# A recurrence over 2048 steps on one core: set-up reordered, first and last chunk's products spread

## What is computed

```python
xn = layernorm(x)
z  = layernorm(xn) * ln_g + ln_b
z  = z + depthwise_conv3(z)                       # over time
gate, ig = split(z @ gate_w.T + gate_b)
Bm = (z * sigmoid(ig)) @ B_w.T + B_b              # 64 states
Cm = z @ C_w.T + C_b
A_bar = expm(dt_A * A)                            # 64 x 64
for t in range(2048):
    s = layernorm(s @ A_bar + Bm[t]) * st_g + st_b
    y[t] = Cm[t] * s
g = silu(xn @ W.T + b + (xn @ V_r) @ C.T)
out = x + (y @ D_w.T + D_b) * sigmoid(gate) * g
```

## Time and profile before

| | us |
|---|---|
| median of 3 runs (lowest, highest) | 2497.48 (2494.24, 2498.33) |
| the profiled execution | 2498.52 |
| its span, first to last instruction | 2496.7 |
| busy: PE, DVE, POOL, ACT | 2455.1, 2187.8, 1239.9, 1013.1 |

### The profile page before, as it was taken

The page is one execution under the profiler, slowest core; times in us unless marked ns, Lnnn a source line. Parts: engine busy times, 40 slices in busy tenths (PEclk is TensorE's granted clock), DMA queues, the critical chain, the costliest instruction groups (busy, mean ns, idle before and its releaser), DMA issues.

```text
span 2496.7 us, 42418 instructions
## 1 busy us (share of the span) xinstructions
PE 2455.1 (98%) x10031; PEld 1313.3 (53%) x10031; DVE 2187.8 (88%) x10934; ACT 1013.1 (41%) x1859; POOL 1239.9 (50%) x2433
## 2 busy tenths in 40 slices
PE   8999999999999999999999999999999999999996
PEld 4555555555555555555555555555555555555544
DVE  5788889988889988899988899888899888899886
ACT  4444433444434443434443434443334444344310
POOL 1445555545555545555445555445555455555443
PEclk9999999999999999999999999999999999999997
DMA  3112212122112122112122112122112122111121
GB/s 112 24 43 59 51 39 53 48 52 60 45 39 58 49 51 60 43 41 55 47 55 60 43 41 55 48 55 60 42 41 52 49 58 59 39 44 52 31 59 36
DMA packets 99542, 125.14 MB, mean 50 GB/s; under 512 B 31967, under 2 KB 48479, under 8 KB 99296
## 3 DMA queue, kind: packets, MB, share of 16 engines
q1 hardware_dynamic: 98560, 121.25, 19.7%
q10 hardware_dynamic: 736, 1.18, 0.2%
HBM read 71.96 MB, written 33.55 MB: 42 GB/s over the span
## 4 chain that ended last, share of the span: by engine, by line
PE 43%; POOL 28%; DVE 20%; issue 8%; ACT 0%; DMA 0%; SPq 0%; POOLq 0%; DVEq 0%; ACTq 0%
POOL dw L428 25%; PE bank L1243 9%; DVE wq L934 8%; PE bank L1232 7%; PE bank L1222 7%; DVE dw L961 6%; DVE dw L947 5%; PE bank L1309 5%; PE bank L1310 4%; POOL ln L455 3%; PE bank L1253 2%; PE bank L1271 2%; PE bank L1262 2%; PE bank L1182 1%; PE bank L1198 1%
## 5 line engine op out<-in xcount | busy, mean ns | idle before, releaser
L428 POOL TENSOR_TENSOR dw<-q,minus_half 8x1 f32<-8x1 f32 x2048 | 1085.7, 530 | 1190.4 <-DVE wq L934 1157.4
L1309 PEld LDWEIGHTS bank<-Mscan,wT 128*65 128x65 f32 x2046 | 228.0, 136 | 618.1 <-issue 607.0
L1232 PE MATMUL bank<-xnorm,gateT 128*128 128x512 f32 x1024 | 507.5, 594 | 0.9 <-DVE sgT L887 0.9
L934 DVE SCALAR_TENSOR_TENSOR wq<-dw 8x65 f32<-8x65 f32 x2048 | 443.2, 216 | 70.2
L1243 PE MATMUL bank<-xnorm,gateT 128*128 128x512 f32 x1024 | 503.3, 597 | 0.0
L1222 PE MATMUL bank<-xnT,WT 128*128 128x512 f32 x1024 | 494.5, 593 | 0.0
L1309 PE MATMUL bank<-Mscan,wT 128*65 128x128 f32 x2046 | 404.4, 279 | 14.0 <-DVE wT L964 11.8
L1310 PE MATMUL bank<-Mscan,wT 128*65 128x128 f32 x2046 | 392.4, 274 | 0.0
L961 DVE SCALAR_TENSOR_TENSOR dw<-dw 8x64 f32<-8x64 f32 x1024 | 279.3, 273 | 111.4 <-POOL dw L428 85.7
L951 DVE SCALAR_TENSOR_TENSOR dw<-bank,dw 8x128 f32<-8x128 f32 x1024 | 342.7, 335 | 12.8 <-PE bank L1310 10.4
L947 DVE SCALAR_TENSOR_TENSOR dw<-dw 8x64 f32<-8x64 f32 x1024 | 279.4, 273 | 77.4 <-POOL dw L428 75.6
(11 more groups left out here) (188 smaller groups left out, 2746.0 us busy)
## 6 DMA issues: line engine op xcount, KB each, us to landing
xc<-in_x SPq DMA_DIRECT2D x252, 128.0 KB, 2.8
xa<-in_x SPq DMA_DIRECT2D x252, 128.0 KB, 2.7
out<-o SPq DMA_DIRECT2D x248, 128.0 KB, 2.4
dw<-dtok SPq DMA_DIRECT2D x127, 96.0 KB
wtok<-dw SPq DMA_DIRECT2D x128, 33.0 KB
gateT<-in_gateT SPq DMA_DIRECT2D x1, 2048.0 KB
WT<-in_WT SPq DMA_DIRECT2D x1, 1024.0 KB, 7.6
xa<-in_x SPq DMA_DIRECT2D x4, 256.0 KB
```

Of the source, the lines that this page charges most:

```text
L428: nc.gpsimd.tensor_tensor(dw[0:B, t, CR:CR + 1], q[:], minus_half[0:B, 0:1], ALU.pow).then_inc(s["r_ready"], 1)
L934: V.scalar_tensor_tensor(out=wq[:], in0=w_eps, scalar=1.0 / S, in1=w_eps, op0=ALU.mult, op1=ALU.mult, accum_out=q[:]).then_inc(s["q_ready" ...
L1232: ins = mm(mbank["gate", m][:], gateT[:, k, P * m:P * m + P], xnorm[p][:, k, :], start=(k == 0), stop=(k == KH - 1))
L1309: mm(scanP[0:WIDE, 0:2 * S], wT[:, 0:WIDE], Mscan[:, 0, :], start=True, stop=False)
```

## The change

In set-up, x's statistics for chunk 0 leave the series and follow its last link; two operations on the small vectors, a memset and a copy move behind the fourth squaring; W's additions take other places; the low-rank products and the halo's transposes swap banks, so that the transposes of z wait for W's additions in place of the halo's copies; the last two of x's four transposes and their copies move behind the squarings. The second to fourth groups of first slots move into steps 0 and 1 of chunk 0, the small product of the first quarter to step 1, b_rest to steps 2 to 5, fill_d to step 6; the other places of chunk 0 move by two (the gate's stay at 44 to 59). On ACT normalise_z(2) moves ahead of copy_dT_rest. In the last chunk last_mm of the third quarter is cut in two halves at steps 57 and 58, and the last quarter's output goes out in two halves, the first on SP's queue, the second on ACT's. Nothing is computed differently.

```diff
-PE_Z_FIRST = (6, 6, 8, 8)
-V_CONV_FIRST = range(9, 25)
+PE_Z_FIRST = (8, 8, 10, 10)
+V_CONV_FIRST = range(11, 27)
-PE_FFN_FIRST = range(5, 21)
-PE_C_FIRST = (21, 22, 23, 24)
-PE_X_FIRST = (18, 18, 23, 23)
-PE_IG_FIRST = range(25, 41)
-PE_B_FIRST = (41, 42, 43, 45)
-PE_D_FIRST = (48, 51, 54, 58)
-V_XG_FIRST = (31, 32, 35, 36, 39, 40, 43, 44)
+PE_FFN_FIRST = range(7, 23)
+PE_C_FIRST = (23, 24, 25, 26)
+PE_X_FIRST = (18, 18, 25, 25)
+PE_IG_FIRST = range(27, 43)
+PE_B_FIRST = (43, 44, 45, 47)
+PE_D_FIRST = (50, 53, 56, 60)
+V_XG_FIRST = (33, 34, 37, 38, 41, 42, 45, 46)
-PE_BREST0 = (0, 0, 1, 1)
-PE_D0 = (3, 3, 3)
+PE_SLOTS0 = (0, 0, 1)
+PE_BREST0 = (2, 3, 4, 5)
+PE_D0 = (6, 6, 6)
-DVE_WPRIME = (2, 3, 3, 4)
+DVE_WPRIME = (1, 1, 2, 3)
-PE_X0 = (10, 10, 12, 12)
+PE_X0 = (10, 10)
-        wbank = [banks[3 + k] for k in range(KH)]
-        hbank = [banks[n] for n in (7, 1, 2, 3)]
+        wbank = [banks[n] for n in (3, 4, 1, 2)]
+        hbank = [banks[n] for n in (7, 3, 4, 5)]
...
-            send_last(3)
+            sp.wait_ge(s["last_add"], 2 * NQ - 1)
+            sp.dma_start(out[:, T - QT:T, 0:H // 2], z[:, NQ - 1, 0:H // 2]).then_inc(s["last_out"], 16)
...
-            for k in range(KH):
+            for k in range(2):
                 copy_xnT(0, k)
             for m in range(KH):
                 input_gate(0, m)
+            for k in range(2, KH):
+                copy_xnT(0, k)
...
             for u in range(DIRECT // 2):
                 copy_first_slots(u)
+            copy_dtok_first()
+            normalise_z(2)
             copy_dT_rest()
-            copy_dtok_first()
+            copy_dtok_second()
             copy_dtok(0, 1)
-            normalise_z(2)
...
+            act.wait_ge(s["last_add"], 2 * NQ)
+            act.dma_start(out[:, T - QT:T, H // 2:H], z[:, NQ - 1, H // 2:H]).then_inc(s["last_out"], 16)
...
-            bn_stats(1, 0, 0)
             dve.wait_ge(s["pe_setup"], 6)
...
-            bn_stats(1, 0, 1)
             dve.wait_ge(s["pe_setup"], 7)
             link(V.tensor_copy(XX[:, 1, :], scanP[0:S, 7 * S:8 * S]))
-            bn_stats(1, 1, 0)
-            bn_stats(1, 1, 1)
-            vec_op(5)
-            vec_op(6)
-            V.memset(ys[S:WIDE, :], 0.5)
-            V.tensor_copy(Dcat[0:S, 0:S], ident[0:S, 0:S])
+            for j in range(2):
+                for h in range(2):
+                    bn_stats(1, j, h)
             for n in range(SQUARINGS):
...
                 if n == 0:
                     for h in range(2):
                         bn_stats(1, 2, h)
+                    bn_stats(1, 3, 0)
                 if n == 1:
-                    for h in range(2):
-                        bn_stats(1, 3, h)
+                    bn_stats(1, 3, 1)
                     aggregate(1)
+                if n == 3:
+                    vec_op(5)
+                    vec_op(6)
+                    V.memset(ys[S:WIDE, :], 0.5)
+                    V.tensor_copy(Dcat[0:S, 0:S], ident[0:S, 0:S])
...
             def fill_z(c, k, i, middle):
                 wait_for(pe, "z_done", NJ, c + 1, NJ)
-                wait_bank(pe, T_USERS, "z", k, i, middle)
+                if c == 0 and k < 2:
+                    pe.wait_ge(s["wprime_done"], k + 3)
+                else:
+                    wait_bank(pe, T_USERS, "z", k, i, middle)
...
-            pe.wait_ge(s["xnT_done"], KH)
+            pe.wait_ge(s["xnT_done"], 2)
...
             mm(scanP[0:S, 4 * S:5 * S], MT[:], M, start=True, stop=True).then_inc(s["pe_setup"], 1)
+            pe.wait_ge(s["dve_setup"], SETUP_M + 4)
+            for k in range(2, KH):
+                fill_x(0, k, -1, False)
             b_first(3)
...
-            for u in range(1, DIRECT // 2):
-                first_slots(u)
...
+                            for u in range(1, DIRECT // 2):
+                                if PE_SLOTS0[u - 1] == t:
+                                    first_slots(u)
+                            if t == 1:
                                 first_quarter_rest()
...
-                        if t in PE_SSM_LAST:
+                        if t in PE_SSM_LAST[:2]:
                             last_mm(PE_SSM_LAST.index(t))
+                        if t == PE_SSM_LAST[2]:
+                            last_mm(2, range(KH // 2))
+                        if t == PE_SSM_LAST[2] + 1:
+                            last_mm(2, range(KH // 2, KH))
```

More of the change, by code:

```diff
@@ L105 @@
 PE_Z0 = (4, 4, 5, 5)
-DVE_STATS1 = (0, 0, 1, 1)
-DVE_WPRIME = (2, 3, 3, 4)
+DVE_WPRIME = (1, 1, 2, 3)
 DVE_CONV = (5, 6, 7, 9)
@@ L196, in build @@
         names = """held consts vec_ready bt_in gate_in vc_in weights_in halo_in xa_in xc_in dve_cleared pool_cleared pe_setup dve_setup halo_zeroed wprime_mm wprime_done bt_steps
-            hmean_done hvar_done b0_mm dT0_done dfirst_mm dfirst_done q0_done
+            hmean_done hvar_done b0_mm dT0_done dfirst_mm dfirst_done q0_mm q0_done
             p_ready r_ready w_ready q_ready wT_ready rest_ready a_ready
@@ L410, in _ @@
             send_last(2)
-            send_last(3)
+            sp.wait_ge(s["last_add"], 2 * NQ - 1)
+            sp.dma_start(out[:, T - QT:T, 0:H // 2], z[:, NQ - 1, 0:H // 2]).then_inc(s["last_out"], 16)
             for name in OUT:
                 sp.wait_ge(s[name], 16 * BJ * LAST)
-            sp.wait_ge(s["last_out"], 16 * NQ)
+            sp.wait_ge(s["last_out"], 16 * (NQ + 1))
         @block.gpsimd
@@ L617, in copy_dtok_first, with copy_dtok_second @@
             def copy_dtok_first():
-                act.wait_ge(s["dfill"], 1)
+                act.wait_ge(s["q0_mm"], 1)
                 nc.scalar.copy(dtok[0:B * (QT - DIRECT), 0, :], tbank["d", 0][0:B * (QT - DIRECT), 0:3 * S]
                                ).then_inc(s["q0_done"], 1)
+            def copy_dtok_second():
+                act.wait_ge(s["dfill"], 1)
                 nc.scalar.copy(dtok[:, 1, :], tbank["d", 0][:, 3 * S:6 * S]).then_inc(s["dtok_done"], 1)
@@ L683, in _ @@
             act.wait_ge(s["vec_ready"], VEC_OPS)
-            act.wait_ge(s["wprime_done"], KH)
             for k in range(3):
@@ L1204, in fill_d @@
                     wait_for(pe, "dT_done", 1, c, 1)
+                if c == 0 and q == 1:
+                    pe.wait_ge(s["q0_done"], 1)
                 if q % 2 == 0 or c == 0:
@@ L1281, in last_fill_w, with last_mm @@
                 tp(last_w[q][:, 0:P], wr[:, q, :], ident[:]).then_inc(s["last_wT"], 1)
-            def last_mm(q):
+            def last_mm(q, blocks=range(KH)):
                 wait_for(pe, "last_ys", 1, q, 1)
@@ L1289, in last_mm @@
                     wait_for(pe, "last_sg", 2, q - 2, 2)
-                for m in range(KH):
+                for m in blocks:
                     ins = mm(last_ssm[q][:, P * m:P * (m + 1)], DT[:, P * m:P * (m + 1)], ys[:, P * q:P * (q + 1)],
                              start=True, stop=True)
-                ins.then_inc(s["last_ssm"], 1)
+                if blocks[-1] == KH - 1:
+                    ins.then_inc(s["last_ssm"], 1)
             def last_fill_o(q):
@@ L1315, in fill_halo @@
                 pe.wait_ge(s["z_done"], NJ)
-                if k == 3:
-                    pe.wait_ge(s["wprime_done"], 1)
+                if k in (1, 2):
+                    pe.wait_ge(s["wprime_done"], k)
                 for j in range(NJ):
@@ L1414, in _ @@
             mm(scanP[0:B, 0:2 * S], vT[:], Dcat[0:S, S:], start=True, stop=True).then_inc(s["p_ready"], 1)
-            for u in range(1, DIRECT // 2):
-                first_slots(u)
             def first_quarter_rest():
                 mm(tbank["d", 0][0:B * (QT - DIRECT), 0:3 * S], dT[:, B * DIRECT:P], Dcat[:],
-                   start=True, stop=True)
+                   start=True, stop=True).then_inc(s["q0_mm"], 1)
             def iteration(i, p, parts, middle):
@@ L1436, in iteration @@
                                     b_rest(k)
-                            if PE_D0[0] == t:
+                            for u in range(1, DIRECT // 2):
+                                if PE_SLOTS0[u - 1] == t:
+                                    first_slots(u)
+                            if t == 1:
                                 first_quarter_rest()
```

## The result

| us | kernel before | changed kernel |
|---|---|---|
| median (lowest, highest), 10 runs each | 2495.17 (2493.03, 2498.33) | 2489.02 (2487.98, 2491.04) |
| the profiled execution | 2498.52 | 2491.04 |
| its span | 2496.7 | 2489.2 |

The ratio is 0.9973 with the interval 0.9965 to 0.9981: 6.15 us less, 0.25%. The ten runs of the kernel before have a median 2.3 lower than the three that the prediction had.

A forecast was written before the change was run, and what follows sets the result against it. The prediction took the recurrence of 2048 steps as the bound, no engine alone. Its terms, 1.15 + 0.87 + 3.5 - 1.45 - 0.1 + 0.95 + 0.4 = 5.3, off the profiled 2498.52 gave 2493.2 us, range 2489.5 to 2497.5.

The forecast's parts named there:

- Statistics and banks: Set-up: earlier statistics of x and swapped banks bring make_y to 27.2; gain 1.15 us (bounds 0.3 and 1.3).
- x's transposes: Set-up: one pair of transposes moves from the squarings into PE's 1.17 wait; gain 0.87 us (bounds 0.2 and 0.9).
- Chunk 0's start: Loop start: slots run fast and DVE's 3.67 wait at t=2 goes; gain 3.5 us, 2.1 if the clock falls.
- rival B: Loop start: the clock falls again there, 1.4 us lost, giving 2494.6; chance 0.18.
- Chunk 0's crowding: Chunk 0: B's products for chunk 1 overfill the pairs of t=44 and 46; loss 1.45 us (bounds 1.1 and 1.7).
- the last gate's tanh behind fill_d at t=60: Chunk 0: fill_d and its copy push this tanh on ACT onto its due time at t=61; loss 0.1 us.
- Last chunk: Steps 57 to 59: halving the eight records removes DVE's 0.99 wait; gain 0.95 us (bounds 0.6 and 1.0).
- Tail: Final output: the first half's transfer starts earlier; gain 0.4 us (bounds a loss of 0.5 and a gain of 1.5).
- case (A): Whole kernel: the terms as summed, with the same clock luck, 2493.2 us with 1.5 either way; chance 0.41.
- Rival C: Squarings in set-up: the clock comes back sooner, worth 1.7 to at most 3.3 us, giving 2490 to 2491.5; chance 0.24.
- D: Set-up: W's fourth addition holds z's transposes, so banks and statistics give 0.3; 2494.3 to 2496 us; chance 0.11.
- E: Squarings in set-up: the clock stays low and PE becomes the bound; slower, 2498.5 to 2503.2 us; chance 0.06.

The follow-up runs named there:

- e3: The changed kernel with the old banks for the low-rank products and the halo's transposes; 2489.12 us, ratio 0.9978 to the kernel before.
- e4: The changed kernel with x's last two transposes and their copies back in the squarings; 2490.83 us, ratio 0.9984 to the kernel before.
- e6: The changed kernel with the second product of dT for chunk 1 at t=51 in place of 53; 2487.42 us, ratio 0.9968 to the kernel before.
- e8: The changed kernel with the last quarter's output in one transfer on SP's queue; 2489.12 us, ratio 0.9973 to the kernel before.
- e9: The changed kernel with chunk 0's first two dT products at t=49 and 50 and x's transposes one at a time; 2487.73 us, ratio 0.9965.
- e10: The changed kernel once more, unaltered; 2489.83 us, ratio 0.9974 to the kernel before.
- e12: The changed kernel with both halves of the last output issued on SP's queue; one execution, 2494.01 us, beside one of the kernel before at 2493.91.
- e11: The kernel before once more, unaltered, one execution; 2497.13 us.
- e7: The kernel before with only the last chunk's third-quarter last_mm cut in two halves; 2494.37 us, ratio 0.9996.
- e2: The kernel before with only the new statistics order, moved vector operations, W's places and banks; 2491.7 us, ratio 0.9987.
- e1: The kernel before with six idle products on PE just ahead of the first transposes of z; 2494.82 us, ratio 0.9997.
- e5: The changed kernel with the whole set-up of the kernel before; 2495.32 us, ratio 0.9996 to the kernel before.

## Why the prediction was wrong, point by point

**Statistics and banks: 1.15.** make_y came 1.17 earlier, at 27.16 where 27.2 was forecast. The size holds in this pair of profiles; over all of them make_y stands at 26.59 to 27.16 in the nine of the new order and at 28.33 to 28.93 in the four of the old one, 1.6 apart in the mean. The share of the banks in it doesn't hold: e3 has it without them.

**x's transposes: 0.87.** 0.87 between e4 and after, 0.92 counted from make_y. Right.

**Chunk 0's start: 3.5.** The wait of 3.67 is gone as forecast, for the reason given: with the hole filled, the slots ran fast (2.12, forecast 12 x 0.20 = 2.4). e4 shows that the filling is what does it there: without it 1.37 of the wait stays. Over all profiles the twelve slots took 2.12 in seven of seven with the hole filled (after, e3, e6, e8, e9, e10, e12), and 2.77 to 3.80 in six of seven with the hole open, e11 being the exception. So rival B, a fall of the clock at the loop's start, came in none of the seven profiles. But the 3.5 was the price of a slow execution: in e11 the same old code lost only 1.85 over a regular pair at t=2 (4.20 and not 2.35).

**Chunk 0's crowding: -1.45.** The pairs of t=46 and 48 take 3.60 and 2.87, an excess of 1.77, of which 0.59 was there before: -1.2. Right; the forecast named them 44 and 46 by the places on PE, though it had read today's overfull pair, of the same kind, at t=46 on DVE.

**The missed step: -1.77.** The sentence that charged 0.1 for the last gate's tanh behind fill_d at t=60 asked the right question of the wrong user only. fill_d of t=51 had moved to 53 with the rest, while the gate's places stayed; its copy stood ahead of the tanh due at t=53. e6 took the 1.6 back with one number changed. So chunk 0 forecast 79.5 to 81 and got 81.15.

**Last chunk: 0.95.** Pairs of t=58 and 60 together fell by 0.96 (e11 to e10 by 0.89, before to e7 by 0.74). Right where the clock is low at t=57. In e2, which has the product in one piece, it was at 1.00 there, and the timeline has:

```profile
2472.48 1.16 PE L1293 MATMUL bank<-ys,DT 128*128 128x128 f32 x8 [0.77 <-DVE ys L906]
```

Its pairs of t=58 and 60 last 2.36 and 2.34: nothing is left for the halves to gain. So this 0.95, too, is a price of the slow level in one profile.

The remaining 1.5 of the -2.49 in the table are three pairs of before (t=30 to 34) over the same code, where a product took 1.92 and not 1.02; e2, e8 and e12 have such pairs too, the others not. It is no part of the change.

**Tail: 0.4, a mis-sized term; it is 1.1.** The earlier start gave the 0.4 that the forecast had: the first half's issue stands 0.45 behind the sums' start, the single transfer's 0.85. The step that failed was holding that nothing else shrinks, between bounds of -0.5 and 1.5. The same 256 KB also moved in 1.74 in place of 2.46, 151 GB/s and not 107. Why is open: with the halves each of the 256 pieces of data is 1024 bytes and not 2048, and no run has halves with rows left whole. The Trainium skill's sentence in DMA: Bandwidth & Descriptors, "Issuing engines are not separate DMA queues", that concurrent issue saves only the issuing time, is borne out by e12 for the second queue (4.26 against 4.21). I had wrongly let it stand for the halving as well, of which it says nothing.

**The clock: the main failure.** The likeliest case (A) held the slow stretch of the squarings as it was in the earlier trace rows, a fixed part of both kernels ("the changed kernel has the same luck"). The runs show that it is no fixed part: the old order also runs without it (e7), the new one also with it (e9, e12), and it is rarer in the new one. Rival C, its coming back sooner, had a chance of 0.24 and a largest price of 3.3, and it is what the profiles of after, e2, e3, e4, e6, e8 and e10 show, at some 3.6. The reason against it, that ACT paces PE until 30, did not decide. The reason for it, the smaller hole ahead of z's transposes, isn't borne out either: e7 is fast with the hole open, e9 and e12 are slow without one. What tips the clock stays open; three of four against two of nine could still be chance. In the medians C is not worth the whole of it: three of four at 3.9 in the mean, less two of nine at 2.9, are 2.3 (an estimate), near the 2 that the fastest executions give.

**The sum again, with what was measured.** 1.17 + 0.87 + 0.95 + 1.1 = 4.1 of work moved or halved, from 3.1 (the last chunk at the fast level) to 4.5 (1.6 for make_y); chunk 0 between +0.45 (the table) and -1.1 (e10 against e11), depending on the clock at its start before; some 2.3 of clock in the squarings. That is 4.3 to 7.3; measured are 6.15, and the ratio's interval is 4.7 to 8.7. The average share of the clock is an estimate from 13 profiles (all but e1's), and whether it is 1 or 3 stays open.

**The base.** The forecast lay 4.2 above the median, and most of that is no gain that I missed. I made the sum against the profiled execution (2498.52) and held the resulting 2493.2 against three runs with a median of 2497.48. With ten runs the median is 2495.17, so the profiled execution lay 3.35 above it: it has the slow stretch in the squarings (3.65), the 3.67 at t=2 and 1.5 in the last chunk, and other executions of the same code lack these or have less of them. The other 0.85 is the gain, 6.15 and not 5.3. The same sum from the median of ten would have given 2489.9, inside the range. That would have been luck in part: the missed stall (-1.77) and the start of chunk 0, priced at a slow profile, offset the clock (+2.3) and the tail (+0.7).

**The other rivals.** D, that W's fourth addition would hold the transposes of z and leave 0.3: it does end last now, but at 25.94, not later than I placed it (26.4), so it cost nothing. E, slower through a clock that stays low: in none of nine profiles of the new set-up order was the input gate slow beyond 37.4, where the old order's was up to 41.

## What to carry to other kernels

Where a stretch holds a slow-clock price, ask before summing whether that price is a fixed part or the luck of one profile; here one profile of before was taken for the average, and other executions of the same code had both levels. Compare it with the median of many runs before using it as a base. Filling a small hole of PE just ahead of a dense stretch can be worth more than the filler's own time (here 0.87 moved and about 1.1 more behind it, e4). When places of one kind of work move past another kind's, follow each moved item through the in-order queue of the engine that takes its result: the whole loss at t=52 was a copy of 0.48 that stood in front of an operation with a due time, and moving one number brought 1.6 back.

## What was not expected of the hardware

**A clock of 1.00 early in a trace may be no measurement.** In e9 the same products took 2.07 at 31.09 and 33.70, and 1.12 from 39.79 on, but the windows (stretch, length, busy, granted clock) have:

```profile
31.00:34.00 3.00, 3.00 (x9) 1.29 (x8) 2.13 (x6) 3.00 (x5) 0.00 (x0) 1.00 0.02 5
```

The trace of e9 has its first record of the clock at 35.7 and that of e11 at 39.8, just where their products become fast; ahead of the first record the view prints 1.00. Where there are records they agree with the pace: before has 0.50 from 28.84 to 39.08, and its pieces there take 2.07. Early in an execution the duration of a known product is the safer reading.

**The same code meets either level.** The old set-up order had pieces of 2.07 (before, e5, e11) and of 1.10 (e7); behind the same hole of 1.17, the slots took 3.80 (before) and 2.12 (e11).

**A last store in two halves ends earlier, on one queue as on two.** From the sums' start to the end of the span: 5.31 and 5.33 with one transfer of 256 KB, 4.21 and 4.26 with two of 128 KB, on two queues or on one. 0.4 of it is the earlier start of the first half; the rest is that the same bytes moved in 1.74 and 1.77 in place of 2.46.
